# Masks of the first attention's scores: from TensorE matmuls into PSUM to affine selects on GpSimd

## The reference, cut to what matters

```python
idx = jnp.concatenate([sel_idx, own], axis=-1)            # 8 selected blocks and the query's own
diag_m = (jnp.arange(n) % SBLK)[:, None] >= jnp.arange(SBLK)[None, :]
fsim = jnp.where(fmask[:, :, None], fsim, NEG)            # own block causal, others if selected
f_out = jnp.einsum('bhgnj,bhnjd->bhgnd', jax.nn.softmax(fsim, -1), fv)
smask = ((delta >= 0) & (delta <= WIN))[None] & (...)     # delta = query position - key position
ssim = jnp.where(smask[None, None, None], ssim, NEG)
s_out = jnp.einsum('bhgwij,bhwjd->bhgwid', jax.nn.softmax(ssim, -1), vcat)
```

## Time and profile before

| | |
|---|---|
| time, median of 3 runs | 5194.31 us (5193.15 to 5207.76) |
| span of the profiled execution | 5194.3 us |
| first attention within it | its quads run in 200 to 1860 us; before that stand the start-up and the first batch's preparation |
| busy over the whole span | TensorE 83%, VectorE 60%, ScalarE 37%, GpSimd 41% |

### The profile page before, as it was taken

One profiled execution on the slowest core, in us unless ns is written; L12 is line 12 of the kernel. 1 busy time (PEld: TensorE's weight loads), 2 busy tenths in 40 slices (PEclk: granted clock), 3 DMA queues, 4 the chain that ended last, 5 costly groups with the idle time before them and its releaser, 6 DMA issues.

```text
span 5194.3 us, 68756 instructions
## 1 busy us (share of the span) xinstructions
PE 4306.7 (83%) x23426; PEld 2568.9 (49%) x23426; DVE 3097.7 (60%) x7197; ACT 1924.1 (37%) x4453; POOL 2108.6 (41%) x1896
## 2 busy tenths in 40 slices
PE   4698888988889958977668988989898989949995
PEld 1454444544445427745434444445444445537774
DVE  6788887878878844556535556464655555422223
ACT  1144434444344432222124444444444444411111
POOL 1000000000000014331046777776767777848885
PEclk6799999999999979989879999999999999979998
DMA  3122121211211047721131111111111111038888
GB/s 99 24 32 42 18 42 28 32 39 20 41 22 34 14 118 195 206 88 31 70 109 32 50 25 47 25 44 30 40 41 33 49 31 39 21 108 205 204 208 225
DMA packets 332117, 358.53 MB, mean 69 GB/s; under 512 B 177326, under 2 KB 257862, under 8 KB 330902
## 3 DMA queue, kind: packets, MB, share of 16 engines
q1 hardware_dynamic: 280888, 276.81, 20.8%
q0 software_dynamic: 47984, 76.34, 7.2%
q10 hardware_dynamic: 2898, 0.98, 0.1%
HBM read 212.35 MB, written 81.89 MB: 57 GB/s over the span
## 4 chain that ended last, share of the span: by engine, by line
PE 56%; DVE 26%; issue 5%; DMA 5%; POOL 4%; ACT 2%; SPq 1%; another core or an unknown queue 1%; ACTq 0%; DVEq 0%; POOLq 0%
PE PS L2151 6%; PE PS L2119 6%; DVE a_mm L1265 6%; PE PS L2104 6%; PE PS L2134 4%; PE PS L2161 4%; PE PS L914 3%; DMA e_xg<-hrow,e_mt 3%; PE PS L854 2%; PE PS L1611 2%; PE PS L2122 2%; PE PS L881 2%; DVE d_t L2317 2%; PE PS L719 2%; PE PS L2526 2%
## 5 line engine op out<-in xcount | busy, mean ns | idle before, releaser
L2389 POOL TENSOR_SCALAR d_ef<-d_ef,d_zr 128x128 f32<-128x128 f32 (+3 forms) x1024 | 1100.4, 1090 | 204.9 <-DVE d_zr L2333 200.4
L1265 DVE TENSOR_REDUCE a_mm<-PS 128x2 f32<-128x384 f32 (+4 forms) x1152 | 673.2, 610 | 230.8 <-PE PS L858 228.5
L1019 ACT ACTIVATE a_PT<-PS 128x512 f32<-128x512 f32 x896 | 514.6, 602 | 612.6 <-PE PS L892 389.7
L2324 DVE TENSOR_REDUCE d_nm<-PS 128x2 f32<-128x768 f32 (+3 forms) x512 | 420.6, 822 | 478.2 <-PE PS L2122 476.5
L1318 POOL DMA_INDIRECT list<-a_tok,slots x64 | 63.1, 986 | 1548.2 <-ACT a_PT L1019 1508.3
L2202 ACT ACTIVATE d_ef<-PS,d_nm 128x128 f32<-128x128 f32 (+3 forms) x1024 | 528.8, 524 | 358.3 <-DVE d_zr L2333 310.1
L2119 PE MATMUL PS<-d_k,d_q 64*128 64x128 f32 (+3 forms) x2048 | 424.7, 492 | 98.1 <-DVE d_t L2317 67.3
L854 PE MATMUL PS<-a_K,a_Q 96*128 96x192 bf16 (+4 forms) x2048 | 418.5, 283 | 52.4 <-DVE a_mm L1265 22.9
L2134 PE MATMUL PS<-ident,d_ef 128*128 128x128 f32 x2560 | 372.3, 280 | 58.3 <-DVE d_tf L2342 25.1
L2151 PE MATMUL PS<-d_tf,d_vt 128*64 128x512 f32 x1280 | 336.8, 660 | 66.9 <-DVE d_tf L2342 53.1
L2317 DVE TENSOR_TENSOR d_t<-PS,d_rope 128x1024 f32<-128x1024 f32 x160 | 188.4, 1219 | 290.0 <-PE PS L2104 283.4
(11 more groups left out here) (344 smaller groups left out, 7882.5 us busy)
## 6 DMA issues: line engine op xcount, KB each, us to landing
e_we<-in_exp SPq DMA_DIRECT2D x79, 768.0 KB
d_q<-d_rr SPq DMA_DIRECT2D x512, 64.0 KB, 2.0
bc_big<-in_exp SPq DMA_DIRECT2D x63, 384.0 KB
d_k<-d_rr SPq DMA_DIRECT2D x256, 64.0 KB, 2.0
yrow<-bc_ob SPq DMA_DIRECT2D x63, 256.0 KB
a_Q<-scr SPq DMA_DIRECT2D x384, 32.0 KB
scr<-a_qsp SPq DMA_DIRECT2D x24, 384.0 KB, 3.0
acc<-d_zero POOLq DMA_DIRECT2D x2, 4352.0 KB, 38.2
```

The lines of the kernel that those rows point to most:

```text
L1019: e.activation(PT[:, 4 * (n % 2) + q4, :], RS.of(("exp", n, q4))[:, :], ACT.Exp, scale=S0).then_inc(act.sem, act.mark(("exp", n, q4)))
L1265: e.tensor_reduce(mm[:, i % 2, kind, c:c + len(gs)], RP.of(("top", b, u, kind, gs[0]))[:, 0:len(gs) * n].rearrange("p (g k) -> p g k", g=l ...
L2324: e.tensor_reduce(nm[:, n % 7, :], S.of(("exp", n))[:, :, 0:128 * i + 128], AX, ALU.max, negate=True).then_inc(dve.sem, dve.mark(("max", n)))
L2389: e.tensor_scalar(ef[:, n % 7, r, 0:nk], ef[:, n % 7, r, 0:nk], zr[:, n % 7, r:r + 1], None, ALU.mult).then_inc(pool_.sem, pool_.mark(("p" ...
```

## The change

The mask matmuls of the main scores go (those of the probes stay), and with them the constants cmaskT and smaskT. The score matmul is now the last of its bank. After the exponential GpSimd zeroes the masked weights in PT, in place, by affine selects: one for each head of a diagonal quad (keep where query - key >= 0), two for each head of a window quad, the second behind a wait for the first (key not over the query, and not more than 64 before it). `times(n)` waits for the last select of a masked quad in place of the last exponential. GpSimd now follows `steps` as well; the list scatters, 64 as before, are issued after the selects of each window quad, and each masked head waits first for the scatters issued before it.

```diff
+            def masked(n):
+                _, _, i, _, kind, kt, _, _ = quads[n]
+                return kind == 1 or kt == i
...
                     if kind == 0 or i == 0:
-                        masked = kind == 1 or kt == i
-                        mm_ = e.matmul(p[:, :], K6[0:rows, y, kind, hh, 128 * kt:128 * kt + 128],
-                                       Q6[0:rows, 4 * hh:4 * hh + 4, 128 * i:128 * i + 128], start=True, stop=not masked)
-                        mk = smaskT[:, 0, :] if kind else cmaskT[:, :]
+                        e.matmul(p[:, :], K6[0:rows, y, kind, hh, 128 * kt:128 * kt + 128],
+                                 Q6[0:rows, 4 * hh:4 * hh + 4, 128 * i:128 * i + 128], start=True, stop=True
+                                 ).then_inc(pe.sem, pe.mark(("exp", n, q4)))
                     else:
-                        masked, mk = True, smaskT[:, 1, :]
...
-                    if masked:
-                        mm_ = e.matmul(p.rearrange("p (g a) -> p g a", g=4), identb[:],
-                                       mk.unsqueeze(1).to_broadcast([128, 4, 128]), start=False, stop=True)
-                    mm_.then_inc(pe.sem, pe.mark(("exp", n, q4)))
...
-                    e.wait_ge(act.sem, act.at(("exp", n, 3)))
+                    if masked(n):
+                        e.wait_ge(pool_.sem, pool_.at(("kept", n)))
+                    else:
+                        e.wait_ge(act.sem, act.at(("exp", n, 3)))
...
-                             (identb, "identb"), (cmask, "cmask"), (smask, "smask"), (cmaskT, "cmaskT"),
-                             (smaskT, "smaskT"), (wo, "wo0")):
+                             (identb, "identb"), (cmask, "cmask"), (smask, "smask"), (wo, "wo0")):
...
-                for c in range(64):
-                    e.wait_ge(act.sem, act.at(("exp", 3 * c, 3)))
-                    e.indirect_dma_start(D["list"], bass.IndirectOffsetOnAxis(slots[:, c:c + 1], 0),
-                                         tok[:, c // 4:c // 4 + 1], None).then_inc(c_l.sem, c_l.tick(16))
+                def keep(n, w, pattern, base, slope):
+                    e.affine_select(w, w, pattern, ALU.is_ge, 0.0, base, slope
+                                    ).then_inc(pool_.sem, pool_.mark(("kept", n)))
+                def score(n, q4):
+                    _, _, i, _, kind, _, _, _ = quads[n]
+                    if masked(n):
+                        chain(e, c_l)
+                        e.wait_ge(act.sem, act.at(("exp", n, q4)))
+                        w = PT[:, 4 * (n % 2) + q4, :]
+                        g = 8 if kind and i else 4
+                        w, a = w.rearrange("p (g a) -> p g a", g=g), 512 // g
+                        keep(n, w, [[0, g], [1, a]], 128 - a, -1)
+                        if kind:
+                            chain(e, pool_)
+                            keep(n, w, [[0, g], [-1, a]], a - 64, 1)
+                    if kind == 1 and q4 == 3:
+                        c = chained(n) // 2
+                        e.indirect_dma_start(D["list"], bass.IndirectOffsetOnAxis(slots[:, c:c + 1], 0),
+                                             tok[:, c // 4:c // 4 + 1], None).then_inc(c_l.sem, c_l.tick(16))
+                steps(idle, idle, idle, idle, idle, score, idle, idle, idle, idle, idle)
```

More of the change, by code:

```diff
@@ L120, in consts @@
     c["cmask"] = cm.astype(bf)
-    c["cmaskT"] = np.ascontiguousarray(cm.T).astype(bf)
     k = np.arange(256)
@@ L125, in consts @@
     c["smask"] = sm[:, 64:].astype(bf)
[L126 to L130, removed]
     c["identb"] = np.eye(128).astype(bf)
@@ L457, in phase_a @@
             cmask = sb("cmask", [128, 128], BF16)
-            cmaskT = sb("cmaskT", [128, 128], BF16)
             smask = sb("smask", [128, 192], BF16)
-            smaskT = sb("smaskT", [128, 2, 128], BF16)
             tok = sb("tok", [128, 32], U32)
@@ L889, in score @@
                                      K6[0:rows, y, kind, hh, k0:k0 + 128],
-                                     Q6[0:rows, 4 * hh:4 * hh + 4, k0 + 64:k0 + 128], start=(x == 0), stop=False)
-                    if masked:
-                        mm_ = e.matmul(p.rearrange("p (g a) -> p g a", g=4), identb[:],
-                                       mk.unsqueeze(1).to_broadcast([128, 4, 128]), start=False, stop=True)
-                    mm_.then_inc(pe.sem, pe.mark(("exp", n, q4)))
+                                     Q6[0:rows, 4 * hh:4 * hh + 4, k0 + 64:k0 + 128], start=(x == 0), stop=(x == 1)
+                                     ).then_inc(pe.sem, pe.mark(("exp", n, q4)))
                     if hh == 7 and kind == 1:
```

## The result

The changed kernel takes 5289.05 us (median of 4 runs, 5281.77 to 5291.62) against 5193.73 us: 1.017 of before, 95% interval 1.0158 to 1.0183. It is slower by 95 us. The forecast was slower by 256, with the select at 1.27 us; the sign was right and the size was not. The profiled execution spans 5285.3 us.

What follows compares the result with a forecast made beforehand. In the first attention TensorE and VectorE were taken to alternate, TensorE slightly slower. 298 - 70 - 70 + 35 + 60 = +253 us on 5194.3 us gave 5447, rounded to 5450 us; range 5130 to 5950.

Steps and rivals of the forecast that it cites:

- the edge: First attention: multiplies wait for GpSimd's last select; stalls of 281 us in window quads and 17 us in diagonal ones.
- the freed slots: TensorE: 512 mask matmuls removed, 112.6 us of slots; 320 inside window quads counted, -70 us.
- VectorE's catching up: During stalls VectorE works off filled banks, so TensorE's waits for it shrink: a third of 222 us idle, -70 us.
- turn-taking: First attention: TensorE and VectorE take turns, TensorE the slower by a little, idle 27.7 us of a 218 us batch.
- the quick rival: Rival: selects of 0.75 us or less nearly fit the window quads' time; 5130 to 5178 us, chance 0.22.
- The price of the select: GpSimd: one affine select on 128x512 f32 taken as 1.27 us, between ends of 0.46 and 2.86 us.
- only i = 2 stays short: Quick rival's claim on window quads: at 0.75 us or less, eight selects lack time at i = 2 alone.
- Scatters: List scatters moved behind window quads' selects land 2.5 us after issue; the wait for them was put at nothing.
- Contention: GpSimd slows 736 VectorE instructions with two SBUF inputs by 0.15 us each, 110 us, a third on the path: +35 us.
- Clock: TensorE's half clock level is granted more with stalls of 4 to 5 us, a tenth of the stage more: +60 us.
- the point of 0.85 us: Select time near which stalls were to balance the freed slots, where the quick rival decides.
- the estimate of 5165 at 0.77 us: Quick rival's time, some 5165 us, if a select takes the Trainium skill's 769 ns for 512 elements.

Runs made afterwards that it cites:

- e15: The changed kernel without selects, without any mask on the main scores and without the wait for selects, on the division's chip: 1.0016 of before.
- e3: The kernel before, its mask matmuls kept, with GpSimd's selects and the multiply's wait for them added: 1.0266 of before.
- e12: The kernel before with the mask matmuls left out at i = 0, 1 and 2 (384 of 512): 1.003 of before.
- e16: The changed kernel with its selects on a spare tile nobody reads, multiply waiting for the exponential alone, masks left out, on the division's chip: 1.0059 of before.
- e14: The changed kernel itself, unchanged, run again on the division's chip: 1.0179 of before.
- e9: The changed kernel with four filler matmuls ahead of each wait for a window quad's selects at i = 1 to 3: 1.0137 of before.
- e4: The changed kernel with one filler matmul ahead of each head's main score at i = 0: 1.0174 of before.
- e10: The kernel before with twelve filler matmuls ahead of the wait of the projection's transposes, from the second batch on: 1.0000 of before.
- e7: The changed kernel without the wait for scatters, each multiply moved behind the next quad's last head: 1.0192 of before.

## Why the prediction was right and wrong

**In short.** +256 us was forecast, +95 came. Three terms of the sum failed: the edge with its price of a select, put at 298 us; the freed slots, put at -70; and VectorE's catching up, put at -70. The mechanism of the edge was right.

**What bounds the kernel.** The reading of turn-taking held, and its consequence was drawn too mildly. TensorE's busy 87% was read as worth relieving. By itself it was not: with 113 us of slots gone the kernel without masks is as slow as before.

**The freed slots.** The sum had 320 of 512 slots as -70 us, and the quick rival all of them as -113. Measured: +8 us for all of them alone (e15), and some -45 once the edge is there (e3 against the changed kernel). This step decided the quick rival; e12 shows it apart from any wait and any select. The trace had the warning in it: the earlier trace rows show the clock at 0.69 in a stretch where TensorE was busy 9.3 of 15 us, and the clock's records have some half clock in 25 of the stage's 32 stretches. I used that for the stalls' price alone, and not for the removed work.

**The price of the select.** 1.27 us against 0.678 measured, min 0.624. In microseconds this is the largest error of the sum. The nearest row by data flow, TENSOR_SCALAR at 1568 ns, was the wrong neighbour, as was TENSOR_TENSOR. The Trainium skill ("GPSIMD Engine Reference", Elementwise — side-by-side cycle accounting) has 769 ns for 512 elements as the best case of a tight loop without branching; this instruction, 657 ns in the median, is quicker.

**The edge.** 281 + 17 us at 1.27 us. The same reading of the same spans at 0.678 us gives some 63 us; the trace has 72 us of pauses, 12 of them behind scatters. The mechanism and its size were right, once the select's price is put right. Its places are all 32 window quads at i = 2 and 3, 9 of 16 at i = 1, and one at i = 0; "only i = 2 stays short" was wrong. The means hid it: at 0.678 us a window quad needs 6.0 us, less than the mean span of 6.37, but in the second half at i = 1 and 2 the kernel before has 4.4 and 3.9 us only, and 10.1 and 5.1 in the first.

**Scatters**, put at nothing: wrong, since the first quad of a batch comes right behind the last one of the batch before, and the landing there is 6.5 us. The pauses behind it are 12 us; the kernel's time fell by some 10 without the wait, within the noise.

**Contention**, +35 us: 22 us measured (e16 against e15). VectorE's busy time in the stretch rose by 50 us (1314.70 without selects to 1365.21 in the row below), in the line with two SBUF inputs among others, as forecast; what it costs the kernel is the 22 us. Were exclusion met at every such instruction, which the forecast drew from the Trainium skill ("SBUF — State Buffer", Who interferes with whom) at +91 us, it would be at the select's real length, as an estimate, 0.33 x 0.34 x 736 = 83 us of VectorE's time; the 50 us lie under that. The row is of the kernel with the selects aside (windows view).

```profile
198.50:1889.30 1690.80, 1412.08 (x8947) 771.68 (x8945) 1365.21 (x3630) 719.83 (x1315) 583.39 (x824) 0.89 0.17 29
```

**VectorE catching up in stalls**, -70 us: too much. With the edge on top of the masks (e3) TensorE's waits for the reductions are 33.3 + 29.7 + 18.2 = 81.2 us, beside 35.2 + 23.5 + 22.9 = 81.6 in the earlier trace rows: they didn't shrink. From the selects aside (e16) to the changed kernel (e14) all of TensorE's waits that VectorE ends fell from 231 to 212 us. So some 20 us, at most.

**Clock**, +60 us for a tenth of the stage more at half: 207 us more came, an eighth of the stage. The removed work alone brings 191 us of it and the edge with its selects alone 138, so it can't be laid to the stalls, as the forecast did.

**The rivals.** The quick select was the case that came, at 0.678 us, under the point of 0.85 us where it was to decide faster from slower. The rival's own terms don't bear that point out: with stalls of 63 us they give 5194 - 113 + 63 + 35 + 15, which is 5194, no change, at 0.678 us, and slower at 0.85; the estimate of 5165 at 0.77 us has the same gap. Against no change the kernel was slower by 95, nearly all of it in the slots, which didn't pay 113 - 35 = 78 us but cost 8. That the forecast's sign was right is luck in this part: two errors, a select twice too dear and slots that were thought to pay, lay on opposite sides. The range, 5130 to 5950, held the time only since it was drawn over both.

**What was to show it.** A mean under 0.85 us was to mean that I am wrong in sign; it didn't, and that pointed to a wrong term. The clock under 0.94, waits of L909 for GpSimd in window quads (86 us of the 300), L1292's length (L1286 in the profile after, source view below: 301 ns on the mean, longest 531) all came. VectorE's wait for the probes rose from 218.4 to 254.5 us, half of the 72 us of pauses.

```profile
L1286 DVE TENSOR_TENSOR a_acc<-a_acc,a_to x128: 291/292/531, 214.5 to 1953.6; 128x128 f32<-128x128 f32 x128
```

**What stays open.** Time at half clock and idle time go together, and the slope alone doesn't say which brings which. That the clock is the cause and not only a companion rests on fillers that made a kernel faster (e9) and on removed work that made one slower (e12), each by 0.3 to 0.4%; two other placings of fillers (e4, e10) changed nothing. e9 and the changed kernel never ran on one chip. Where a filler helps can't be told beforehand from these runs. Nor was it settled why the masks' removal wins 45 us beside the edge and nothing without it, or why a multiply that stands later in the order (e7) is reached no later.

## What to carry to other kernels

Before work is taken off TensorE, look at its granted clock in the stage: where it stands a little under 1.00, as 0.94 here, the freed slots may come back as time at half clock. Test a removal alone, with nothing in its place, before building its replacement. Look for the shortest spans at an edge, not for their mean. When an edge is put from one engine through another, its cost is set by the time from the first input to the asker, against what the new chain needs, and not by the other engine's free share: GpSimd was free for 96% of the stage, and the edge through it still cost 62 us.

## What the runs showed of the hardware

An affine select on 128x512 f32 in place takes 624 ns at the least, 657 in the median and 678 on the mean of 768, less than half of TENSOR_SCALAR on the same shape (1568 ns). Removing 384 matmuls of 0.22 us with nothing else changed makes this kernel slower by 0.3% (e12), its granted clock 0.90 for 0.94. Four useless matmuls ahead of each of 48 multiplies, which wait about 1.1 us on the mean, make the changed kernel faster, 1.0137 for 1.017, its clock 0.92 for 0.89 (e9). VectorE's 128x128 add with two SBUF inputs, 292 ns with GpSimd silent, has 339 ns on the mean and 559 at the longest with GpSimd busy a third of the time on a tile of its own, and 301 and 531 in the changed kernel. A scatter of one column of tokens from GpSimd lands after 2.1 to 8.8 us, 2.5 in the median; in the changed kernel those issued at a batch's start take 4.9 to 6.9 us, and five of those issued some 90 us later 7.8 to 8.7.
